# Moving one more group of the shared expert from the last block into the block that assigns slots

## The reference

```
x = x + tanh(g_xattn) * attention(layernorm(x), context)
xn = layernorm(x)
shared = (silu(xn @ Wg_s) * (xn @ Wu_s)) @ Wd_s           # two shared experts, 256 wide each: 512 together
comb   = the two largest softmax(xn @ router_w), divided by their sum
routed = sum over the 2 chosen of 16 experts: comb * ((silu(xn @ Wg_e) * (xn @ Wu_e)) @ Wd_e)   # 128 wide
x = x + tanh(g_ffn) * (shared + routed)
```

## Time and profile before

| | |
|---|---|
| median of 3 runs | 2094.84 us (2093.85 to 2103.59) |
| profiled execution, its own time | 2091.02 us |
| its span | 2089.1 us |
| PE busy / PE weight loads | 93% / 72% of the span |
| DVE / ACT / POOL busy | 54% / 37% / 60% |
| mean granted PE clock | 0.972 of full speed |
| PE clock per fortieth of the span, from the 27th slice | 8 6 7 9 8 9 9 8 9 9 9 9 9 9 tenths |

### The profile page before, as it was taken

The page is one execution under the profiler, slowest core; times in us unless marked ns, Lnnn a source line. Parts: engine busy times, 40 slices in busy tenths (PEclk is TensorE's granted clock), DMA queues, the critical chain, the costliest instruction groups (busy, mean ns, idle before and its releaser), DMA issues. The chain is left out here.

```text
span 2089.1 us, 40601 instructions
## 1 busy us (share of the span) xinstructions
PE 1935.3 (93%) x12484; PEld 1503.2 (72%) x12485; DVE 1119.3 (54%) x1763; ACT 772.2 (37%) x1533; POOL 1248.9 (60%) x1398
## 2 busy tenths in 40 slices
PE   1899999999999999999999999998779799999799
PEld 1777878778787787877878777785468566666687
DVE  3465655655656565565655556565347233333476
ACT  1144444444445454444444444444222122221000
POOL 3277776777767777677776867766524233333531
PEclk9999999999999999999999999998679899999899
DMA  6646548375583745738466383664063454445864
GB/s 164 184 126 178 156 127 243 98 193 144 137 231 94 212 129 152 202 110 223 115 167 188 112 236 101 180 168 129 27 237 89 159 164 145 147 146 162 230 188 135
DMA packets 170481, 330.43 MB, mean 158 GB/s; under 512 B 20279, under 2 KB 69431, under 8 KB 169671
## 3 DMA queue, kind: packets, MB, share of 16 engines
q1 hardware_dynamic: 156724, 286.95, 48.8%
q0 software_dynamic: 10880, 33.56, 6.0%
q10 hardware_dynamic: 2832, 9.33, 1.2%
HBM read 214.17 MB, written 115.14 MB: 158 GB/s over the span
## 5 line engine op out<-in xcount | busy, mean ns | idle before, releaser
L835 DVE TENSOR_REDUCE neg_max<-score 112x1 f32<-112x750 f32 x512 | 480.4, 938 | 564.5 <-PE score L1105 563.3
L613 ACT ACTIVATE probs_t<-st 125x448 f32<-125x448 f32 x768 | 414.1, 543 | 519.4 <-PE st L1131 515.3
L470 POOL TENSOR_TENSOR acc<-acc,probs_t 125x448 f32<-125x448 f32 x256 | 309.5, 1209 | 64.8 <-ACT probs_t L613 63.0
L1069 PE MATMUL proj<-ctx_hi,weights 128*128 128x376 f32 (+1 forms) x1024 | 331.2, 349 | 10.2 <-POOL parts L425 9.7
L1131 PE MATMUL st<-q_stack,k_stack 98*125 98x224 f32 x1536 | 334.2, 301 | 6.4 <-DMA q_stack<-shift_rows 3.2
L472 POOL TENSOR_TENSOR acc<-acc,probs_t 125x448 f32<-125x448 f32 x256 | 300.1, 1172 | 20.1
L1131 PEld LDWEIGHTS st<-q_stack,k_stack 98*125 98x125 f32 x1536 | 267.8, 191 | 60.8 <-issue 28.5
L1105 PE MATMUL score<-k_stack,q_stack 96*112 96x512 f32 (+1 forms) x1024 | 284.2, 359 | 20.2 <-DVE neg_max L835 13.0
L462 POOL TENSOR_TENSOR acc<-probs_t 125x448 f32<-125x448 f32 x128 | 146.2, 1143 | 173.8 <-PE pv L1157 154.3
L1079 PE MATMUL proj<-weights,ctx_hi 128*125 128x512 f32 x768 | 246.8, 402 | 0.0
L1069 PEld LDWEIGHTS proj<-ctx_hi,weights 128*128 128x128 f32 x1024 | 192.7, 190 | 36.5 <-issue 18.2
(11 more groups left out here) (209 smaller groups left out, 2766.9 us busy)
## 6 DMA issues: line engine op xcount, KB each, us to landing
k_stack<-k_parts SPq DMA_DIRECT2D x192, 375.0 KB, 6.3
ctx_raw<-in_ctx_t SPq DMA_DIRECT2D x64, 375.0 KB, 9.9
k_parts<-k_hi SPq DMA_DIRECT2D x64, 375.0 KB, 6.6
k_parts<-k_lo SPq DMA_DIRECT2D x64, 375.0 KB, 7.2
y_slots<-y_sb SPq DMA_DIRECT2D x72, 256.0 KB, 2.9
q_stack<-q_parts SPq DMA_DIRECT2D x64, 224.0 KB, 4.1
gu_sb<-in_w_gu ACTq DMA_DIRECT2D x4, 2048.0 KB, 17.6
x_in<-in_x SPq DMA_DIRECT2D x16, 448.0 KB, 8.9
```

Source lines behind the costliest of these rows:

```text
L470: nc.gpsimd.tensor_tensor(both, both, tiles(c, p, pair, 0), ALU.add).then_inc(half_added, 1)
L613: act.activation(probs_t[0:KW, (c * PHASES + p) % 2, u % HC, :], st[u % 2][0:KW, 0:2 * L], ACT.Exp)\
L835: nc.vector.tensor_reduce(neg_max[:, h // HC % 2, h % HC, t:t + 1], score[0:QW, 0:S], axis=AX.X, op=ALU.max, negate=True).then_inc(maxed, 1)
L1069: ins = nc.tensor.matmul(bank[:, 0:w], wp[:, d, c * P:(c + 1) * P], xp[:, d, at:at + w], start=(d == 0 and k == 0), stop=(d == DC - 1 and ...
```

## The change

HEAD goes from 3 to 4. The fourth group's shared expert (g = 3) is put behind everything else in the streams of the slots block: POOL's `columns_low(3, d)` behind the last `hot_tiles`, ACT's part behind `hidden_high(2, 3)`, DVE's behind the line that writes `slot_token` and behind `finish(2)`, PE's behind `down(2, j)`. The last block has four heavy groups and four light ones. Three light groups are completed one group late, as before, and the fourth by DVE in the last heavy group, behind the third. Where SP stores the light groups is changed to fit.

```diff
-HEAD = 3
+HEAD = 4
...
                 columns_low(2, d)
             for n in range(4, CHUNKS):
                 hot_tiles(n)
+            for d in range(DC):
+                columns_low(3, d)
...
             silu(2, 3)
             hidden_high(2, 3)
+            for d in range(DC):
+                columns_high(3, d)
+            for j in range(SC):
+                silu(3, j)
+                hidden_high(3, j)
...
             finish(2)
+            hidden(3, 0)
+            for j in range(1, SC):
+                hidden_low(3, j - 1)
+                hidden(3, j)
+            hidden_low(3, SC - 1)
+            finish(3)
...
             for j in range(SC):
                 down(2, j)
+            for j in range(SC):
+                gate_up(3, j)
+            for j in range(SC):
+                down(3, j)
...
-                if 1 <= s <= HEAD:
-                    l = s - 1
-                    sp.wait_ge(light_done, s)
+                for l in () if s == 0 else (s - 1, s) if last else (s - 1,):
+                    sp.wait_ge(light_done, l + 1)
...
-                    if 1 <= g <= HEAD:
+                    if g:
                         light(g - 1, j)
+                if last:
+                    for t in range(GT):
+                        light(HEAD - 1, t)
```

## The result

| | before | changed |
|---|---|---|
| median of 5 runs | 2094.84 us (2093.85 to 2103.59) | 2106.05 us (2103.89 to 2109.79) |
| profiled execution, its own time | 2091.02 us | 2105.65 us |
| its span | 2089.1 us | 2103.9 us |
| slots block's end: POOL's first instruction behind it | 1644.93 us | 1672.58 us |
| last block's start: the same | 1915.01 us | 1942.89 us |

The ratio, taken over all runs, is 1.0047, with a 95% interval of 1.0029 to 1.0066: 0.47% slower, as forecast (2104.7 us). The interval lies wholly above 1, so the slowdown is real, though it is under the 0.5% that the forecast had as its line between a change and none. The medians differ by 11.2 us (0.54%), the two spans by 14.8, since the profiled execution of before lay 3.8 us under its median. The terms are read from the spans.

The account below looks back on a forecast made before the run. The last block was taken as bound first by the columns' transfer, then by PE. Terms 30.75 - 3.5 - 30.67 + 8.0 + 5.3 = +9.9 us on the 2094.84 us median gave 2104.7 us, range 2098 to 2111 us.

Parts of the forecast that it names:

- The two PE terms: PE's matmuls for one group: +30.75 us added in the slots block, -30.67 us taken from the last block, cancelling.
- The slots block's end: Slots block: d_sb lands under the new group, so the last stores find free engines, -3.5 us.
- Rival 1's second form: Slots block's end not shortened, on top of the 10.2 us wait: sum +13.4, 2108.2 us; 0.25 for both forms.
- rival 4: Slots block: the new group starts late, gap at most 9.4 us, sum +19.3, 2114.2 us; chance 0.02.
- Rival 3's clock: Behind the slots block: a shorter pause might keep PE's clock up, saving 1.6 us at restart; chance 0.04.
- DVE's tail: Last heavy group: five light pairs before the routed rows, 7.25 us less 1.92 us of pause, +5.3 us.
- "I take +8.0 us": Last block: PE's wait for the second heavy group's columns grows by one load of light rows, +8.0 us.
- "a longer pause adds nothing to that": Last block: PE's clock is already at 1.2 GHz behind the wait for columns, so restart adds nothing.
- its own sign: Last block: the prediction is wrong if the pause for columns stays near 13 us or exceeds 23; 20.8 expected.
- Rival 1's price by all of the added bytes: Last block: all added bytes pass before the columns, wait +10.2 us, sum +12.1, 2106.9 us; 0.25 for both forms.
- rival 2: Last block: the wait for columns hardly grows, 6.2 us or nothing, sum +8.1 or +1.9; chance 0.12.

Follow-up runs that it names:

- the pair of profiles: Kernel before and changed kernel, both unchanged, run again on the first chip for second profiles: 2105.12 us and 2120.24 us, one run each.
- the last kernel: Changed kernel with columns first, light groups 0 and 1 brought in during the first heavy group, 2 and 3 in the next two, operations paired: 2081.04 us, ratio 0.9924.
- the kernel with the paired operations: Changed kernel with light group 3's operations spread over the four j of the last heavy group, beside light group 2's: 2113.40 us, ratio to before 1.0045.

## Why the prediction came out as it did

**The two PE terms** were right: +30.65 against +30.75, with no pause in front of the new group, and one group of the last block is 30.7 us in the changed kernel as well. They cancel.

**The slots block's end** was right in mechanism and nearly in size: -2.9 for -3.5 us. The forecast had taken the median of four stores, 2.5 us, but the end waits for the last, which took 2.9: 3.1 us less than before, and 0.2 are left unexplained. On the first chip the pair of profiles gave 2.8 us, on the second the last kernel and the one with its rows spread 2.4. Rival 1's second form, that the end isn't shortened, is out, and so is rival 4. Rival 3's clock gained nothing either: the first four `turn` took 1.08 us behind the shorter pause and 1.09 behind the longer.

**DVE's tail** was right, +5.1 for +5.3 us, and the kernel with the paired operations showed that it is these pairs: with three fewer in the way the tail was 4.4 us shorter.

**"I take +8.0 us"** for the wait for columns is the term that failed. It measured +11.5, and +0.9 for a slower restart that I had put at nothing ("a longer pause adds nothing to that"). The 0.9 us may be chance and not the longer pause, since the kernel with everything light a group later had as slow a restart (4.81 us) behind a pause of 4.32. The pause of 24.35 us is beyond the 23 at which the prediction said that it would be wrong, so by its own sign it failed here, though its total came out. The fourth load cost about what I said, 8.7 us. What I had left out is that the three loads ahead of it came up to 2.9 us later as well. The reason I gave, that "the gathers come in at their own pace", was right in itself, but it says nothing on how many of their bytes pass before the columns do: 2.02 MB more and not the 1.32 that 8.0 us let in. Rival 1's price by all of the added bytes (10.2 us) was the nearer one and still a little low; rival 2, a wait that hardly grows, is refuted by the 24.35 us. Why the first three loads were delayed isn't settled; SP's queue sent about as many packets in the first 13.7 us (1099 before, 1124 changed), so the bytes seem to have gone to other loads of the same queue.

The Trainium skill, "DMA: Bandwidth & Descriptors", section "Queues, rings and completion order", has the rule that I leaned on, one packet from each queue in turn. The traces agree where both queues are backed up: from 1958.8 to 1975.5 the changed kernel's q0 sent 920 packets and q1 918. Over the whole stretch the added traffic was 703 packets on q0 to 464 on q1. That doesn't refute the rule, but the forecast had used it for this added traffic, and there one to one was wrong. The same section says that completion within one issuing engine's queue isn't first in, first out; that would fit the late landing of the earlier loads, but no run here shows it as the cause. The 4.1 us for 896 KB that rival 2 took from the Trainium skill, "DMA: Bandwidth & Descriptors", section "Anatomy of one DMA", are an estimate by a fit that the page gives for DMAs issued by GpSimd. These loads are SP's, and with little beside them theirs is the 6.2 us of the earlier trace rows.

**That the whole came out at 0.47%, as forecast, is partly luck.** The terms sum to +14.6 us on the spans. The medians differ by less, 11.2 us, because the profiled execution of before lay 3.8 us under its median, and I had added my sum to the median. So two errors went opposite ways: the terms were 4.7 us short (14.6 against 9.9), and the medians moved 3.6 us less than the spans.

**What stays open.** The size of the pause's growth, 11.5 us, stands on one profile of each kernel: the second pair, on the first chip, has no such pause. On the first chip both original kernels lose another 11 to 13 us in the last block to engines that get on slowly while the DMA engines are saturated. The moved parts (rows, gathers, columns) show that it ends with the backlog and not with the columns' landing. They don't show what slows the engines, nor why one chip does it and the other doesn't at the same DMA share. On the second chip it isn't shown which part of the rearrangement brought the gain. The instruction queues (q8 and q14) moved as few packets in both. On that chip the trace also lacks the landings of the last block's loads, so whether the recording itself has a part in it can't be told from these runs. The prediction spoke of none of this. It doesn't turn its sign: there, too, the changed kernel and its variants were 0.2 to 0.6% slower than before.

## What to carry to other kernels

Work that costs an engine the same in two places still drags its by-products with it: here one load, eight gathers and five pairs of vector operations, and these made the whole difference. Where a stage opens with a backlog, price an addition by all the bytes that can pass before the awaited transfer lands, on every queue, and not by one queue's pace: here that gave 10.2 us and one queue's pace 8.0, where 11.5 were measured. Then put the transfer that the bound engine waits for in front, and don't ask for all of the rest at once. On the first chip the order alone was worth nothing and order and spreading together 0.8%; on the second the order with one part of the rest spread was worth 0.8%. Moving the group gained nothing either way: 0.47% slower as it stood, and within 0.1% once the traffic was spread.

## What the runs showed of the hardware

- Under saturated DMA engines (share 1.04 to 1.07, 263 to 274 GB/s) one chip, once that had lasted some 10 to 15 us, let PE start a matmul every 2.1 to 2.8 us instead of every 0.2, ran an ACT instruction 31 us after its input was there, and recovered within 2.5 us of the end of the traffic, while POOL issued a gather every 1.23 us throughout. The first profile of the same kernel, at the same DMA share, has PE at full pace, and so have the kernels on the second chip.
- SP's issue of a load is no small thing in a backlog: the two loads of columns held SP's queue for 18.56 us, where the same two take 1.24 us with only one load ahead of them (the kernel with the rows spread).
- Four stores of 224 KB landed in 6.0 to 6.3 us with a load of 4 MB issued 8 us ahead of them, and in 2.3 to 2.9 us where it was away.
- The first twelve matmuls behind a pause of PE took 4.05 us after 12.82 us idle, 4.82 after 24.35, 4.81 after 4.32 and 3.08 after 2.25: the cost of a restart doesn't grow steadily with the pause.
